# A transformer block with head attention: values laid with heads innermost, twelve heads of the value product on GpSimd, and the normalised input made in the routing

## The reference

```python
# heads: 16 heads of 16, and the softmax runs over the heads of one token
Q, K, V = (xn @ W + b).reshape(B, S, 16, 16)  # for each of Wq, Wk, Wv
score = einsum('bsid,bsjd->bsij', Q, K) / sqrt(16)   # 16 x 16 per token
out = einsum('bsij,bsjd->bsid', softmax(score), V)
# ffn: latent causal attention over 2048 tokens, then 2 of 8 experts
h  = xn + mla(rmsnorm(xn, g1), Wq, Wdkv, Wuk, Wuv, Wo)
ffn = h + moe(rmsnorm(h, g2), gate_w, w1, w2)
```

## Time and profile before

| | us |
|---|---|
| median of three runs | 2916.65 |
| the profiled execution | 2925.71 |
| its span, first to last instruction | 2923.9 |
| TensorE busy in it | 2546.4 (87%) |
| VectorE | 2283.6 (78%) |
| GpSimd | 2180.7 (75%) |
| ScalarE | 1570.9 (54%) |

### The profile page before, as it was taken

The page is one execution under the profiler, slowest core; times in us unless marked ns, Lnnn a source line. Parts: engine busy times, 40 slices in busy tenths (PEclk is TensorE's granted clock), DMA queues, the critical chain, the costliest instruction groups (busy, mean ns, idle before and its releaser), DMA issues. The chain is left out here.

```text
span 2923.9 us, 58265 instructions
## 1 busy us (share of the span) xinstructions
PE 2546.4 (87%) x21356; PEld 1302.0 (45%) x21356; DVE 2283.6 (78%) x3685; ACT 1570.9 (54%) x2357; POOL 2180.7 (75%) x1196
## 2 busy tenths in 40 slices
PE   7999878999999999999999999985672988898893
PEld 4544432333333333333333333224562877777782
DVE  4558758899989998999899988603653899999980
ACT  2322225777777777677777767781221544444441
POOL 4543339798889888988889888993565677778782
PEclk9999999999999999999999999996765999999996
DMA  6785642123323332333223321117864555565555
GB/s 204 255 276 195 221 160 64 48 76 87 81 63 86 86 80 65 84 85 88 60 84 85 89 59 60 43 40 237 283 208 154 120 122 121 114 138 125 124 91 149
DMA packets 252852, 351.78 MB, mean 120 GB/s; under 512 B 30536, under 2 KB 192168, under 8 KB 251816
## 3 DMA queue, kind: packets, MB, share of 16 engines
q1 hardware_dynamic: 224968, 304.32, 35.1%
q0 software_dynamic: 27360, 39.73, 7.9%
q10 hardware_dynamic: 256, 4.19, 0.4%
HBM read 255.35 MB, written 162.43 MB: 143 GB/s over the span
## 5 line engine op out<-in xcount | busy, mean ns | idle before, releaser
L1044 DVE TENSOR_REDUCE p_piece_max<-p_ring 128x1 f32<-128x512 f32 (+3 forms) x2160 | 1293.7, 655 | 137.0 <-PE p_ring L157 67.4
L1102 ACT ACTIVATE p_probs<-p_st 128x1024 f32<-128x1024 f32 (+3 forms) x1280 | 1078.8, 897 | 414.2 <-PE p_st L1165 216.7
L1165 PE MATMUL p_st<-unit_q,unit_k 64*128 64x512 bf16 (+3 forms) x3520 | 433.1, 348 | 41.6 <-ACT p_probs L1102 24.9
L1183 PE MATMUL p_pv<-p_probs,unit_vg 128*32 128x512 f32 (+3 forms) x3520 | 411.6, 542 | 0.0
L982 POOL TENSOR_TENSOR p_terms<-p_head_p,p_head_in 128x4096 f32<-128x4096 f32 x32 | 348.7, 10897 | 0.1
L1835 POOL DMA_INDIRECT acc<-p_y,p_rows x142 | 223.4, 1573 | 135.8 <-ACT p_y L1963 49.5
L170 PE MATMUL p_ring<-unit_k,unit_q 64*128 64x512 bf16 (+3 forms) x1600 | 271.6, 352 | 27.9 <-DVE p_piece_max L1044 25.4
L961 POOL TENSOR_TENSOR p_terms<-p_head_in 128x4096 f32<-128x4096 f32 x32 | 283.2, 8850 | 8.4 <-POOL p_head_s L969 4.4
L2000 PE MATMUL p_y_ps<-p_w,p_hid 128*128 128x256 f32 x1136 | 278.9, 402 | 11.1 <-ACT p_hid L1951 10.8
L1818 POOL TENSOR_TENSOR p_pv<-p_pr,p_qkv 128x1280 f32<-128x1280 f32 (+2 forms) x78 | 259.6, 3328 | 26.8 <-ACT p_q_ps L1943 26.8
L988 POOL TENSOR_TENSOR p_terms<-p_terms 128x2048 f32<-128x2048 f32 (+2 forms) x96 | 252.2, 2627 | 17.1 <-POOL p_terms L988 11.4
(11 more groups left out here) (187 smaller groups left out, 3477.4 us busy)
## 6 DMA issues: line engine op xcount, KB each, us to landing
p_w<-ffn_w SPq DMA_DIRECT2D x142, 512.0 KB
qk_parts<-p_parts SPq DMA_DIRECT2D x64, 384.0 KB, 3.4
head_qkv<-p_heads SPq DMA_DIRECT2D x16, 1536.0 KB, 6.7
p_rows<-rows_by_expert SPq DMA_DIRECT2D x71, 258.0 KB, 3.4
unit_q<-qk_parts SPq DMA_DIRECT2D x132, 128.0 KB, 3.2
unit_k<-qk_parts SPq DMA_DIRECT2D x132, 128.0 KB, 3.6
v_padded<-p_vx SPq DMA_DIRECT2D x16, 1024.0 KB, 8.2
p_head_in<-head_qkv SPq DMA_DIRECT2D x32, 384.0 KB, 3.8
```

The lines of the kernel that those rows point to most:

```text
L1044: nc.vector.tensor_reduce(piece_max[:, n % 2, h:h + heads, i, pc], ring_ps[g % RING][:, 0:heads * width].rearrange("p (h k) -> p h k", h=h ...
L1102: nc.scalar.activation(probs[:, 2 * turn_of(s, i) + u, :, 0:width], st_ps[u][:, :, 0:width], ACT.Exp).then_inc(probs_done, 1)
L1165: last = nc.tensor.matmul(st_ps[u][:, half, 0:width], k6[s][rows, PAIR * second + u, kt * P:(kt + 1) * P], q6[s][rows, PAIR * second + u, ...
L1183: last = nc.tensor.matmul(pv_ps[hh * VW:(hh + 1) * VW, skip:CT], vg[s][:, kt, hh * VW:(hh + 1) * VW], probs[:, 2 * turn_of(s, i) + hh % PA ...
```

## The change

- The value columns of the head projection and their bias are permuted once, at the start, on VectorE (from `rest`, used as staging), so that a value row is laid feature by feature with the heads innermost: column 16 d + j. Both value products then read the value operand with innermost step 1.
- In the experts GpSimd's share goes from 10 to 12 heads (pieces of 6 and 6; 4 and 2 around a pair's DMA), VectorE's from 6 to 4.
- `xn` is neither stored nor loaded. The projections keep two numbers per row (`row_stats`: the inverse deviation, and minus the mean times it), and ScalarE makes `xn` from `x` in the routing (`make_xn`, two chunks ahead, after `ediff`), into two buffers. `add_attention`, which overwrites half of `x`, waits for it (`xn_made`). SP keeps its wait for `xn_done` before it loads over `x`.

```diff
@@ -314,13 +314,11 @@
                 sp.dma_start(g1[:, :], w["ffn_g1"].rearrange("(k p) -> p k", p=P)).then_inc(w_loaded, 16)
-            for i, name in enumerate(("q", "k", "v")):
+            for i, name in enumerate(("q", "k")):
                 sp.dma_start(wh[:, :, i, :], w[f"attn_W{name}"].rearrange("(k p) n -> p k n", p=P)).then_inc(w_loaded, 16)
                 sp.dma_start(bh[:, i, :], w[f"attn_b{name}"].partition_broadcast(P)).then_inc(w_loaded, 16)
-
-            def store_xn(b, c, n):
-                wait_apart(sp, xn_done, n + 1, apart)
-                sp.dma_start(xn_v[b, c], xn[:, c % 2, :, :]).then_inc(xn_stored[c % 2], 16)
+            sp.dma_start(rest[:, 0:KD, 0:D], w["attn_Wv"].rearrange("(k p) n -> p k n", p=P)).then_inc(w_loaded, 16)
+            sp.dma_start(rest[:, KD, 0:D], w["attn_bv"].partition_broadcast(P)).then_inc(w_loaded, 16)
@@ -361,7 +359,7 @@
-                    store_xn(*((b, c + 1) if c + 1 < NC else (b + 1, 0)), n + 1)
+                    wait_apart(sp, xn_done, n + 2, apart)
                     if c + 3 < NC:
@@ -471,12 +468,13 @@
                 dve.wait_ge(rstd_steps, 2 * n + 2)
-
-                dve.wait_ge(xn_stored[s], 16 * u)
                 for t in range(TT):
...
                 last.then_inc(xn_done, 1)
+                nc.vector.tensor_copy(row_stats[:, 0, bass.ds(n * TT, TT)], rstd[:, :])
+                nc.vector.scalar_tensor_tensor(row_stats[:, 1, bass.ds(n * TT, TT)], mv[:, :, 0], -1.0, rstd[:, :],
+                                               ALU.mult, ALU.mult)
@@ -529,6 +527,12 @@
             nc.vector.tensor_scalar(bh[:, 0, :], bh[:, 0, :], DH ** -0.5, None, ALU.mult)
+
+            for k in range(KD):
+                nc.vector.tensor_copy(wh[:, k, 2, :].rearrange("p (d h) -> p d h", h=H),
+                                      rest[:, k, 0:D].rearrange("p (h d) -> p d h", d=DH))
+            nc.vector.tensor_copy(bh[:, 2, :].rearrange("p (d h) -> p d h", h=H),
+                                  rest[:, KD, 0:D].rearrange("p (h d) -> p d h", d=DH))
             for k in range(KD):
@@ -932,7 +936,6 @@
-            sp.dma_start(first_xn[:, :, :], xn_v[0, 0]).then_inc(first_loaded, 16)
@@ -981,7 +984,7 @@
                     terms[:, :, :, :], head_p[:, u, :, :].unsqueeze(2).to_broadcast([P, H, DH, H]),
-                    head_in[:, u, 2, :, :].rearrange("p j d -> p d j").unsqueeze(1).to_broadcast([P, H, DH, H]),
+                    head_in[:, u, 2, :, :].unsqueeze(1).to_broadcast([P, H, DH, H]),
                     ALU.mult), before + 1)
@@ -1242,7 +1246,7 @@
         x = [first_x, *(sb(f"p3_x_in{c}", [P, TT, D]) for c in range(1, NC))]
-        xn = [first_xn, *(sb(f"p3_xn_in{c}", [P, TT, D]) for c in range(1, NC))]
+        xn = sb("p3_xn", [P, 2, TT, D])
         oT = [first_oT, *(sb(f"p3_oT_in{c}", [P, KD, CT]) for c in range(1, NC))]
@@ -1321,7 +1326,7 @@
-        N_LOADED = 16 * 3
+        N_LOADED = 16 * 2
@@ -1347,7 +1352,6 @@
-                sp.dma_start(xn[c][:, :, :], xn_v[b, c]).then_inc(loaded[c], 16)
@@ -1461,13 +1465,14 @@
                 dve.wait_ge(attn_loaded[c], 16 * (b + 1))
+                dve.wait_ge(xn_made, n + 1)
                 nc.vector.tensor_tensor(x[c][:, 0:2, :], x[c][:, 0:2, :], attn[:, c, :, :], ALU.add).then_inc(attn_added, 1)
...
                     nc.vector.tensor_tensor(x2[:, 2 * i:2 * i + 2, :], mla_ps[i][:, :].rearrange("p (t d) -> p t d", d=D),
-                                            xn[c][:, 2 * i:2 * i + 2, :], ALU.add).then_inc(x2_done, 1)
+                                            xn[:, c % 2, 2 * i:2 * i + 2, :], ALU.add).then_inc(x2_done, 1)
@@ -1582,6 +1587,17 @@
         def _(act):
+            def make_xn(b, c, n):
+                act.wait_ge(loaded[c], N_LOADED * (b + 1))
+
+                if not isinstance(n, int) or n >= 2:
+                    act.wait_ge(x2_done, 2 * n - 2)
+                for t in range(TT):
+                    last = nc.scalar.activation(xn[:, c % 2, t, :], x[c][:, t, :], ACT.Identity,
+                                                bias=row_stats[:, 1, bass.ds(n * TT + t, 1)],
+                                                scale=row_stats[:, 0, bass.ds(n * TT + t, 1)])
+                last.then_inc(xn_made, 1)
+
             def squares(n):
@@ -1603,6 +1619,8 @@
+            make_xn(0, 0, 0)
+            make_xn(0, 1, 1)
             squares(0)
@@ -1611,6 +1629,8 @@
                 nc.scalar.activation(ediff[:, :], diff[:, :], ACT.Exp).then_inc(ediff_done, 1)
+                if ahead >= 2:
+                    make_xn(*after(b, c + 2), n + 2)
                 if ahead >= 1:
@@ -1693,12 +1713,12 @@
-    HP = 10
+    HP = 12
...
-    PIECES = {2: (5, 5), 3: (4, 3, 3)}
+    PIECES = {2: (6, 6), 3: (4, 4, 4)}
@@ -1818,7 +1838,7 @@
                     pr[:, u, heads, :].unsqueeze(2).to_broadcast([P, count, DH, H]),
-                    qkv[:, m % QB, 2, :].rearrange("p (j d) -> p d j", d=DH).unsqueeze(1).to_broadcast([P, count, DH, H]),
+                    qkv[:, m % QB, 2, :].rearrange("p (d j) -> p d j", d=DH).unsqueeze(1).to_broadcast([P, count, DH, H]),
                     ALU.mult)
```

More of the change, by code:

```diff
@@ L269, in phase1_project @@
         vx_done = sem("p1_vx_done")
-        xn_stored = [sem(f"p1_xn_stored{s}") for s in range(2)]
         parts_stored = [sem(f"p1_parts_stored{s}") for s in range(2)]
@@ L1300, in phase3_route @@
         x2_done = sem("p3_x2_done")
+        xn_made = sem("p3_xn_made")
         ss_done = sem("p3_ss_done")
```

15 lines of the change are left out of this document (8 added, 7 removed).

## The result

The changed kernel takes 2888.95 us, the median of four runs (2883.59 to 2892.92), against 2916.49 for the kernel before in the same set of runs: a ratio of 0.9904, 95% interval 0.9887 to 0.9922, or 28 us less. The forecast was 2870.6, 46 us less, in a range of 2852 to 2898. The profiled execution took 2890.86 us (span 2889.0).

The account below looks back on a forecast made before the run. VectorE was taken to bound the experts, with GpSimd nearly as full. Experts -47, change of stage -4, first loads -6, projections -2, `xn` +10 and small work +3 gave -46 us: 2879.7 profiled, 2870.6 median, range 2852 to 2898.

Parts of the forecast that it names:

- The change-over: End of the attention: GpSimd's shorter products let the last `head_o` and the loads behind it come earlier, -4 us.
- the first loads: Start of the routing: without `xn` loads ahead, the small loads VectorE waits for come earlier, -6 us (-2 to -8).
- the projections at -2 + 3: Projections: TensorE's wait for the unit's last transfer goes, -2 us; permuting copies and small per-chunk instructions cost +3.
- Rival E: Routing: ScalarE's Identity needs table loads, two a chunk, +36 us on top of the forecast, 2907 us; chance 2 in 100.
- so both engines want 16.1 to 16.2: Experts: VectorE and GpSimd each need 16.1 to 16.2 us a block instead of 17.68, so the stage loses 47 us.
- TensorE, at 14.9, does not bind: Experts: TensorE alone would want 14.9 us a block, below the other engines' 16.2, so it sets no limit.
- twelve heads pay off under 0.79 us a head: Experts: moving from ten to twelve heads on GpSimd gains only while a head costs it under 0.79 us.
- Rival D: Experts: GpSimd becomes the bound; at 0.85 us a head +21 us, the whole 2939 us; chance 6 in 100.
- rival B: Experts: VectorE's product stays at 1.80 ns an element, so the stage gains 29 us, the whole 2888; chance 7 in 100.
- A: Experts: GpSimd's price falls half as much, to 0.73 us a head; the stage gains 22, the whole 2896; chance 12 in 100.
- +10 for `xn` in the routing: Routing: VectorE's add waits for ScalarE's `xn`, about 1.1 us in 9 of 14 chunks, +10 us (0 to +22).
- rival C: Routing: `xn` costs nothing or even gains from lighter DMA; the whole -58 us, 2858 us; chance 11 in 100.

Follow-up runs that it names:

- e5: The kernel before, unchanged, profiled again beside the following runs; 2929.51 us.
- e6: The changed kernel, unchanged, run again on the same chip as e5; 2903.40 us, ratio 0.9918 to the kernel before.
- e7: The changed kernel with longer rings in the experts: six buffers for rows and outputs instead of four, four for blocks instead of three; ratio 0.9876 to the kernel before.
- e12: e11 with eleven heads on GpSimd instead of twelve, five on VectorE; ratio 0.9856 to the kernel before.
- e4: The changed kernel with GpSimd's share back at ten heads instead of twelve; 2897.36 us, ratio 0.9881 to the kernel before.
- e8: The changed kernel with the longer rings of e7 and ten heads on GpSimd instead of twelve; ratio 0.9871 to the kernel before.
- e9: The kernel before with twelve heads on GpSimd instead of ten, nothing else; 2935.65 us against 2916.88, ratio 1.0055.
- e10: The kernel before with three one-element memsets added to VectorE's program ahead of the routing's loop; 2905.08 us, ratio 0.9963.
- e11: The changed kernel with e7's rings and, around the pair's adding DMA, 3 heads before and 5 behind instead of 4 and 2; 2865.23 us, ratio 0.9821.

## Why the forecast was right and where it was wrong

**Right**: the sign, the range, the instruction prices but that of `xn`, and the total up to the routing. The change-over and the first loads were put at -4 and -6, the projections at -2 + 3. The attention starts 0.5 us earlier, and the rows that answer to the earlier trace rows are

```profile
1964.89 0.36 SPq L901 DMA_DIRECT2D attn_rows<-p_head_o  x1
...
1983.19 0.69 DVE L1469 TENSOR_TENSOR first_x<-first_x,p_attn 128x512 f32<-128x512 f32 x1 [9.93 <-DMA p_gate_w<-ffn_gate_w]
```

The last `head_o` reaches SP 4.65 us earlier (-4 forecast), and the wait for the small loads falls from 13.45 to 9.93 (-3.5; -6 forecast, -2 the bound). Together -9 forecast, -8.0 in the first pair of profiles and -10.8 in e5 and e6. In the projections TensorE's wait for its last transfer did not shorten (4.31 to 4.09 us), so that -2 did not come, but neither did the +2 of the small work. Rival E did not come: the changed kernel's table loads are the 65 of the experts (`L1971` and `L1962`) and one in the projections, none in the routing.

**Wrong: the step "so both engines want 16.1 to 16.2, and the experts lose 32 x (17.68 - 16.2) = 47 us."** 6.5 to 9.5 us came. Both needs were nearly right. Over the whole window GpSimd waited for ScalarE 24.6 + 14.8 us in 14.6 periods before, 2.7 us a period, so it needed 35.55 - 2.7 = 32.85 for four tiles; the single period of the earlier trace rows, with its wait of 3.03, gave 32.33. After, it waits 7.7 + 21.0 us in 14.9 periods and needs 34.85 - 1.9 = 32.9, against 32.4. What failed is that the larger of two mean needs was taken for the period. It is the period of about half the blocks; in the others a delay goes round the circle of four engines with its short rings: VectorE waits 3.1 us a period for GpSimd, GpSimd 1.9 for ScalarE, TensorE 4.0 for rows. "TensorE, at 14.9, does not bind" rested on the earlier trace rows, the stage's first tiles, whose rows had been loaded ahead; in the steady state it waited for rows already in the kernel before, 53.5 us of it, with VectorE full beside it. That cover was the forecast's to name, and with it what SP waits for ahead of the rows. The runs give the shares of what is missing: 11 us by longer rings (e7 against e6), 11.5 more with the pair's DMA covered and eleven heads (e12 against e7). Of the remaining 15, 32 x 0.27 = 9 are what the eleven heads themselves cost, since VectorE then needs 16.4 us a block in place of 16.13; some 6 are the late blocks that are left, and their cause is open.

**Wrong: twelve heads pay off under 0.79 us a head.** A head costs 0.66, and twelve are still slower than ten by 0.23 to 0.37% (e4 against the two sets of the changed kernel, whose intervals it touches in one and misses in the other), 7 to 11 us; with the long rings they are level (e7, e8). The threshold compared the changed kernel with the kernel before, not with the layout alone, which already took VectorE to 16.66 us a block; from there GpSimd was the engine to relieve. Rival D's condition, a head at 0.79 us or more, did not come here; e9 has it and loses. The nearest times are those of rival B, 2888, and A, 2896, by prices (1.80 ns an element on VectorE, 0.73 us a head) that did not come: that B's number is within 1 us of the measured one is chance.

**Wrong: +10 for `xn` in the routing.** The wait is there and longer than forecast (1.6 us a chunk, for 588 ns in place of 405), but with the load that is saved it costs nothing, which is rival C's condition: VectorE had 24.0 / 9 = 2.7 us of wait for GpSimd's inverse root behind it in each chunk, and GpSimd's list is what sets the period where nothing stalls. The forecast counted nine of 14 chunks, and its ground was that GpSimd was seen waiting 6.04 us for the squares in the earlier trace rows. The profile of e10 has no such wait in its window: it came with VectorE's stalls. The routing then gained 12 us on the lower level and 5 on the upper, in place of the 10 that it was to lose, by the place of the loop. Without that accident the change would have been worth some 17 us on the lower level, that is 2900 us: the sign would have held, but the time would have stood at the edge of the forecast's range, 2 us outside it. That it fell well inside is luck: of the two errors, -47 for -6.5 and +10 for -12, the second gives back half of the first.

## What to carry to other kernels

When the bound of a stage is cut, the next period is at least the larger of the remaining needs, and longer where a ring is short: list every wait that is hidden under the bound today, with its total, and ask of each ring (buffers, queues, landings) how far ahead it runs. Cost a joint edit against each of its parts alone, since the part that gained may need the other least. And where an engine stands in a loop for several microseconds with no releaser, move its code by a few instructions before anything is concluded from a difference of that size.

## What the runs showed of the hardware

Three one-element memsets ahead of a loop are worth 11 us (0.9963, 0.9950 to 0.9975): VectorE's stalls of 4.5 to 5.5 us at two neighbouring instructions of the loop (e9) go, and the instruction queue carries 3 packets instead of 13 in 140 us. With an innermost step of 16 floats in the value operand in place of 1, VectorE's product takes 2761 ns against 1748 for 1536 elements and 1904 against 1214 for 1024, GpSimd's 10897 against 8853 for 4096 and 4746 against 3951 for 1536. `xn`, an activation with its scale and its bias from columns at a moving place, takes 588 ns for 128x256, against 405 for a square of the same shape; in a row, four take 2.08 us. GpSimd's scatters land 3.9 us after their issue in the median, and up to 8.1 us after it beside a load of new weights (e11). Sets of runs on different chips differ by 12 us in this kernel (2916.5 to 2916.9, 2928.1 to 2929.7), and the profiles of the upper level alone have VectorE's waits of 22.1 to 32.7 us at `p_place`; why is open.
